# Regrouping the low products of the first pass: pairs behind every second step instead of one behind each step

## What is computed

```
x = x + L0_ffn(L0_cond(x))       # x: 64 samples x 64 tokens x 1024
x = x + L1_ffn(L1_cond(x))
L0_cond: y[b] = x[b] mixed over its 64 tokens by W[condition[b]] (64 x 64)
L0_ffn:  y @ W_base.T + b_base + routed low-rank term (8 experts, rank 16, top 2)
L1_cond: x[b] @ weight[adapter_ids[b]].T          # 8 matrices of 1024 x 1024
L1_ffn:  16-fold sum over 8 experts of softmax(router) * (x @ A.T) @ B.T, rank 16
```

## Time and profile before

| | |
|---|---|
| median of 3 runs | 720.71 us (719.87 to 720.83) |
| the profiled execution | 720.81 us |
| its span, first to last instruction | 719.1 us |
| granted TensorE clock | 1.00 |
| PE busy | 711.3 us, 99% |
| DVE busy | 402.1 us, 56% |
| ACT busy | 115.7 us |
| POOL busy | 57.8 us |
| bytes moved | 156.26 MB, 217 GB/s on average |

### The profile page before, as it was taken

The page is one execution under the profiler, slowest core; times in us unless marked ns, Lnnn a source line. Parts: engine busy times, 40 slices in busy tenths (PEclk is TensorE's granted clock), DMA queues, the critical chain, the costliest instruction groups (busy, mean ns, idle before and its releaser), DMA issues.

```text
span 719.1 us, 12198 instructions
## 1 busy us (share of the span) xinstructions
PE 711.3 (99%) x4448; PEld 638.3 (89%) x4448; DVE 402.1 (56%) x1092; ACT 115.7 (16%) x312; POOL 57.8 (8%) x115
## 2 busy tenths in 40 slices
PE   8999999999999999999999999999999999999998
PEld 8999987898889988898889888998889888989997
DVE  2000298067846576466826784657646782685544
ACT  2222300031103110021003110311002100320111
POOL 1222310001100000001000110000000100010100
PEclk9999999999999999999999999999999999999999
DMA  8999993406755377428724674547742872386462
GB/s 301 413 369 345 390 412 105 170 5 207 250 197 198 124 230 268 172 80 302 278 113 151 210 255 190 196 129 230 263 175 76 303 273 118 147 304 222 180 249 88
DMA packets 38340, 156.26 MB, mean 217 GB/s; under 512 B 8852, under 2 KB 10900, under 8 KB 28052
## 3 DMA queue, kind: packets, MB, share of 16 engines
q1 hardware_dynamic: 27026, 78.66, 29.0%
q0 software_dynamic: 9216, 71.31, 28.8%
q10 hardware_dynamic: 2050, 5.65, 2.0%
HBM read 133.24 MB, written 22.35 MB: 216 GB/s over the span
## 4 chain that ended last, share of the span: by engine, by line
PE 92%; DVE 5%; DMA 2%; issue 1%; SPq 0%; ACT 0%; POOLq 0%; DVEq 0%
PE base_ps L387 17%; PE base_ps L388 17%; PE base_ps L389 17%; PE base_ps L401 10%; PE low_ps L461 4%; PE out_ps L461 4%; PE mix_both L415 4%; PE mix_both L426 3%; PE out_ps L415 2%; PE low_ps L415 2%; DVE w_lo L772 1%; PE low_ps L426 1%; PE out_ps L426 1%; DMA adapter<-folded 1%; PE mix_both L428 1%; PE low_ps L387 1%
## 5 line engine op out<-in xcount | busy, mean ns | idle before, releaser
L387 PE MATMUL base_ps<-yT,w_hi 128*128 128x512 f32 (+1 forms) x576 | 212.4, 369 | 0.7 <-DVE xT L916 0.5
L389 PE MATMUL base_ps<-yT,w_hi 128*128 128x512 f32 (+1 forms) x576 | 211.5, 367 | 0.0
L388 PE MATMUL base_ps<-yT,w_lo 128*128 128x512 f32 (+1 forms) x576 | 211.5, 367 | 0.0
L387 PEld LDWEIGHTS base_ps<-yT,w_hi 128*128 128x128 f32 x576 | 108.6, 188 | 20.7 <-DVE xT L916 2.7
L389 PEld LDWEIGHTS base_ps<-yT,w_hi 128*128 128x128 f32 x576 | 108.5, 188 | 17.8
L388 PEld LDWEIGHTS base_ps<-yT,w_lo 128*128 128x128 f32 x576 | 108.5, 188 | 16.0
L1079 POOL DMA_DIRECT2D adapter<-folded x60 | 31.9, 532 | 555.1 <-PE low_ps L461 482.8
L401 PE MATMUL base_ps<-ag_raw,stage 128*128 128x136 f32 x640 | 74.6, 280 | 0.6 <-DMA stage<-in_w 0.5
L401 PEld LDWEIGHTS base_ps<-ag_raw,stage 128*128 128x128 f32 x640 | 74.3, 190 | 1.0 <-DMA stage<-in_w 0.7
L776 DVE TENSOR_TENSOR yT<-mix_both,yT 128x512 fp32r<-128x512 f32 x32 | 22.0, 691 | 87.9 <-ACT yT L649 87.9
L955 DVE TENSOR_TENSOR xT<-xT,low_ps 128x512 f32<-128x512 f32 (+1 forms) x31 | 20.5, 662 | 87.9 <-PE low_ps L389 87.9
(11 more groups left out here) (197 smaller groups left out, 904.8 us busy)
## 6 DMA issues: line engine op xcount, KB each, us to landing
adapter<-folded POOLq DMA_DIRECT2D x63, 1088.0 KB, 5.5
stage<-in_w SPq DMA_DIRECT2D x39, 512.0 KB, 6.3
x_rows<-in_x SPq DMA_DIRECT2D x32, 512.0 KB, 8.7
xT<-in_x_turned SPq DMA_DIRECT2D x16, 1024.0 KB, 6.0
out<-xT SPq DMA_DIRECT2D x28, 512.0 KB, 2.7
folded<-adapter ACTq DMA_DIRECT2D x10, 544.0 KB, 6.4
w_raw<-in_w SPq DMA_DIRECT2D x8, 256.0 KB, 6.8
w_raw<-in_w SPq DMA_DIRECT2D x4, 512.0 KB, 12.6
```

Of the source, the lines that this page charges most:

```text
L387: pe.matmul(dst, st_hi, mv_lo, start=start, stop=False, skip_group_check=True)
L388: pe.matmul(dst, st_lo, mv_hi, start=False, stop=False, skip_group_check=True)
L389: return pe.matmul(dst, st_hi, mv_hi, start=False, stop=stop, skip_group_check=True)
```

## The change

In rounds 1 to 6 the samples' low products are placed behind other base steps of the first pass: 0 and 1 behind step 1, 2 and 3 behind step 3, 4 and 5 behind step 5, 6 behind step 6 and 7 behind step 7. Behind the steps 0, 2 and 4 none stands. In round 7 the order remains as it was. The instructions, their number and their waits are the same; only PE's order changes. The lists of DVE, ACT, POOL and SP stay word for word.

```
-                    if l1:
-                        if k < 2:
+
+
+                    samples = (k,) if toks == A else ((), (0, 1), (), (2, 3), (), (4, 5), (6,), (7,))[k]
+                    for i in samples if l1 else ():
+                        if i < 2:
                             pe.wait_ge(hg_copied, at(q, r, TILES, TILES))
-                        make_low(q, r - 1, k, low_banks)
+                        make_low(q, r - 1, i, low_banks)
```

## The result

The changed kernel takes 726.85 us in the median of 6 runs (725.66 to 728.54), the kernel before 720.34 us in 6 runs beside them. The ratio is 1.0093, with a 95% interval of 1.0082 to 1.0104. The forecast was 727.4 us, which is 1.0093 times the 720.71 us it started from. The profiled execution took 726.39 us with a span of 724.7 us.

The account below looks back on a forecast made before the run. PE was taken to bound the kernel, with its second pass waiting for DVE's add_base. Low 4, 2.65 us late less 0.46 and 1.11 us idle, leaves about 1.11 us; six rounds add 6.7 to 720.71: 727.4 us, range 725.4 to 730.4.

Parts of the forecast that it names:

- The sum: Rounds 1 to 6: add_base on DVE 1.11 us late per round, 6.7 us in all, giving 727.4 us.
- PE's own gain: First pass of rounds 1 to 6: three base steps at 2.73 instead of 2.77 us, saving 0.12 us a round.
- The cost of a low product right behind another: On PE, within each pair: taken as zero; at most 0.23 us per pair, which would give 730.1 us.
- The boundaries on DVE: In front of x1T_low(7) and sum_low(7): no early start assumed; if both save 0.08 us, delay 0.95 and 726.4 us.
- the bounds: On the 727.4 us: 726.4 if both DVE boundaries save 0.08 us, 730.1 if a second low product costs 0.23 us.
- No adapter was late: Rival, 7%: low 3's adapter takes 7.8 us against 6.5 of room, PE stands 1.3 us a round, 735.2 us.
- The chain on DVE did not shrink: Rival, 4%: x1T_low(6) to add_base runs without pauses, the 1.11 us vanish, 720.0 us.
- this rival: Clock falls, 2%: after PE's 1.3 us pause one base step runs at 1.2 GHz, 2.73 us a round, 743.8 us.

Follow-up runs that it names:

- both moves: PE's order as in the change, with turn_hw(0 to 3) behind sum_low(0 to 3) and add_base ahead of sum_low(7) on DVE: 717.27 us, ratio 0.9969 to the kernel before.
- the run with pairs 0 to 3: Changed kernel, but low products 4 and 5 one by one behind their own steps, only 0, 1 and 2, 3 paired: 721.64 us, ratio 1.0025.
- the run with later adapters: Changed kernel, but in rounds 1 to 6 the adapters of samples 3 to 7 are asked for one low product later: 739.56 us, ratio 1.0275.

## Why the prediction was right

Each step of the working, as an offset from the start of round 3's first base step, beside the changed kernel's rows (those above, and `add_base` at 352.62):

| step | predicted | measured |
|---|---|---|
| low 0 | 5.55 | 5.51 |
| low 4 | 20.51 | 20.47 |
| `x1T_low(6)` | 22.14 | 22.11 |
| `x1T_low(7)` | 25.45 | 25.44 |
| `sum_low(6)` | 30.19 | 30.18 |
| `sum_low(7)` | 31.46 | 31.44 |
| `add_base` | 33.41 | 33.39 |
| second pass | 34.2 | 34.20 |
| `delta` | 30.01, and a wait of 0.2 to 0.3 | 30.20 |

- *Where it goes.* The second pass is 34.20 - 33.08 = 1.12 us late in round 3; over the rounds it is 1.10 us each. The sum had 1.11 us. That PE's order costs this through DVE's list, and not by itself, is shown by the runs that leave PE as changed and move only instructions of DVE. With `turn_hw` early the 0.9% is gone and a round is as short as PE's gain makes it; with `add_base` first it is gone against the kernel before, but 0.16 us a round stay against the kernel before with the same move. That low 4 decides is shown by the pair 4, 5 alone, 1.0108.
- *PE's own gain.* Predicted 0.12 us a round and covered by the wait. Uncovered it is 0.10 with `turn_hw` early and 0.13 with both moves.
- *The cost of a low product right behind another.* Zero was taken, 0.23 us was the bound. The starts are 325.74 - 324.74 = 1.00 us apart, and the second product of the pair takes 326.74 - 325.74 = 1.00 us in front of a base step: nothing is added.
- *The boundaries on DVE.* The transposes end at 343.39 + 1.25 = 344.64, and `x1T_low(7)` starts at 344.67, so the 1.25 us counted in full. By the rule for "Two Vector instructions with no wait between them" of the Trainium skill ("VectorE: DVE Perf Modes") it had to be held; the trace agrees. At the other new boundary `sum_low(7)` starts 0.03 us behind the end of `sum_low(6)` (350.35 + 0.29 = 350.64 against 350.67), so that one saved nothing either. The 0.08 us of the bounds do occur elsewhere in the list: `sum_low(0)` ends with the addition L845, 327.99 + 0.29 = 328.28, and `x1T_low(3)` behind it starts at 328.20.
- *The rivals.* No adapter was late in rounds 1 to 6. The chain on DVE did not shrink. The granted clock is 1.00 in the rounds, with pauses of PE of 0.97 us six times. The row held against this rival showed less than the prediction took from it: in the stretch of the earlier trace rows the 1.2 us that PE was not busy are several pauses, the longest of them 0.67 us ahead of a low product at 643.30. So what settles it is the changed kernel's own six pauses.
- *What the working missed*, without harm here: the backlog that low 2 leaves. I used it only as a check that DVE is free at 339.13. It decides as soon as low 4 is not late, and costs 0.24 us a round there.

## What to carry to other kernels

An engine that is half idle can still be the last at one place of a loop. Find that place by the wait that repeats once a round, and measure the engine's slack there by its own idle times, in order, from the moved instruction up to the place: lateness minus the idle times passed on the way is what the round loses. This holds if the engine has no backlog when it reaches the moved instruction; the run with pairs 0 to 3 shows the loss when it has one. Bunching work on the busy engine also bunches the release of its buffers, so count the consumer's whole list behind each release. The cure may be a change of the consumer's order: take what can be done earlier out of the stretch, and put what the busy engine waits for ahead of what nobody waits for yet.

## What the runs showed of the hardware

- After the pause of 2.52 us in the run with later adapters, the granted TensorE clock fell to the 1.2 GHz level for about 3.4 us. Windows of that kernel (us; busy and count of PE, PEld, DVE, ACT, POOL; granted clock, DMA share, GB/s):

```profile
266.00:267.00 1.00, 0.94 (x7) 0.94 (x8) 0.93 (x4) 0.00 (x0) 0.00 (x0) 1.00 0.76 296
267.00:268.00 1.00, 1.00 (x6) 0.88 (x5) 0.50 (x2) 0.64 (x2) 0.05 (x1) 0.80 1.08 435
268.00:269.00 1.00, 1.00 (x4) 0.75 (x3) 0.97 (x3) 0.07 (x1) 0.48 (x1) 0.50 0.67 261
...
271.00:272.00 1.00, 1.00 (x8) 0.88 (x7) 0.31 (x2) 0.62 (x1) 0.00 (x0) 0.99 1.03 418
```

  PE worked again for about 1.5 us at full clock before it fell, and a matmul of 512 columns then came every 0.43 us in place of 0.23 (its start rows run 268.06, 268.49, 268.92). The stretch from low 5 to low 6 took 271.50 - 266.06 = 5.44 us in place of the 344.46 - 340.70 = 3.76 us of the changed kernel's round 3. In the same profile a pause of 2.36 us in round 6 was followed by 592.94 - 589.08 = 3.86 us, so the clock did not fall there. What separates the two is open. The mean granted clock of this kernel's five executions was 0.998, 0.995, 0.992, 0.988 and 0.988, and they took 736.64, 737.28, 739.56, 741.76 and 741.96 us; the profiled one is the first, so the others spent longer at the lower level.
- Two 1088 KB loads asked for 1.3 us apart on the same queue: the first is not slowed (5.3 and 5.4 us to landing in round 3 of the changed kernel), the second takes 7.0 to 7.8. For the pair at the end of a round, asked for 1.45 us apart, it is 5.2 and 8.7 us in the kernel before and 5.3 and 8.8 in the changed one.
- A base step takes 2.77 us right behind a low product and 2.73 behind another base step; why, no run shows. That makes grouping worth 0.04 us for each stretch saved.
